# Attention on one core: value products moved to the end of a half step, projections in one piece, and TensorE's program written out

## The chip, the core and the metric

The kernel runs on one core of a Trainium2 chip. The core has five engines that run side by side and meet through semaphores: TensorE (PE; its weight loads are shown apart as PEld), VectorE (DVE), ScalarE (ACT), GpSimd (POOL) and SyncE (SP, which issues the DMAs). The metric is the time of one execution in microseconds, lower is better. A matmul writes its result into one of eight banks of PSUM, and a bank can be used again only when whoever reads it has read it.

## The reference

64 sequences of 128 positions and 256 channels go through two blocks. Each block is a cross attention and a mixture of experts, each with a residual. The change touches only the two attentions. Cut to what matters, one of them is:

```python
q = (layernorm(x) @ Wq + bq).reshape(B, L, H, D)      # H = 16 heads of D = 16
k = (ctx @ Wk + bk).reshape(B, L, H, D)
v = (ctx @ Wv + bv).reshape(B, L, H, D)
scores = einsum('blhd,bshd->bhls', q, k)              # 128 x 128 for each head
scores = where(mask, -inf, scores)
attn = softmax(scores * scale, axis=-1)
out = einsum('bhls,bshd->blhd', attn, v).reshape(B, L, H * D)
x = x + out @ Wo + bo
```

## The kernel before

**Work and its pieces.** The function `attention` is called twice, once for each block. It goes through 32 steps, `p` = 0 to 31. A step holds two sequences, and is done in two halves, `s` = 0 and `s` = 1, one sequence each. The 16 heads of a sequence are four units of four heads, so that a unit's scores (128 queries by 4 x 128 keys) fill one PSUM bank. Several stages overlap: in step `p` the scores of `p` are made, the queries, keys and values of `p+1` and `p+2` are projected, and the output of `p-1` is projected.

**What a half does on TensorE.** `score` writes the mask of all four units (L534 and L538, bf16, on 32 rows of the array) and adds the score products (L548, 32 rows). `turn_n` (L481) turns the normed input of step `p+2` and stands in half 0 only. `turn_p` (L559) turns one unit's probabilities, four 128x128 transposes into the bank that the unit's scores had. `project_q`, `project_k`, `project_v` and `project_o` are groups of fp32 products in three parts each, written by the helper `mm3` (L69, L70 and L71). `times_v` (L572) multiplies the turned probabilities of a unit with the values, on 32 columns of the array. `turn_recip` (L580) turns the reciprocals of the sums. In half `s` the probabilities' units 2 and 3 of the half before ("the late units") are turned first, then units 0 and 1 of the half itself. The value products in a half are those of the half before.

**What the others do.** DVE: `row_max` (L777) takes the extremes of a unit's scores, `keep_p` (L784) copies a unit's turned probabilities to `probsT`, `invert` (L790) the reciprocals, `rest_n` (L760) the low part of the normed input, `keep_o` (L798) copies the raw output, `keep_v` (L769) the values, `residual` (L805) adds to `x`, `stats` (L812) and, in steps 0 to 6 of the first attention, `measure` (L2582) take statistics of `x`. ACT: `exps` (L693) makes a unit's probabilities and their sums, `round_n` (L671) and `round_c` (L676) the high parts of the inputs, `keep_q`, `keep_k`, `norm` the rest. POOL: `normalize`, `spread`, `rest_c`, `add_bo` and `split_q`, which makes the queries' halves that the scores need.

**What sets the order.** Each engine runs its own list in the order in which it is written; there is no scheduler. An instruction whose semaphore has not come stops all that stand behind it on its engine. ACT's list in a step is `keep_k(p+1)`, `round_n(p+2)`, `round_c(p+2)`, four `exps`, `keep_q(p+1)`, `norm(p+3)`, four `exps`. So the first `exps` of half 0 stand behind `round_n`, which waits for TensorE's `turn_n`. And `turn_n` waits for the `residual` of two steps back, because both use bank 7:

```python
wait(pe, x_done, p - 3)                               # in turn_n
wait(pe, exp_done, UP * p + UNITS * s + (u + 1 if u < 2 else UNITS))   # in turn_p
if u == UNITS - 1:
    wait(pe, pT_ready, UP * p + k)                    # the bank of unit 2, read by keep_p
```

TensorE's list is a loop over steps 10 to 27 in the first attention and 2 to 27 in the second (`pairs`, two steps a turn); the other steps, and all steps of DVE, ACT and POOL, are written out.

Of the kernel before, what the change touches and what calls it, by code (L numbers as in the profile page):

```python
# [26 lines left out]
P = 128  # L27
# [34 lines left out]
def is_(index, value):  # L62

    return isinstance(index, int) and index == value
# [301 lines left out]
def attention(nc, S, L, ctx_dram, W, bias, counted, load_next, signals, first, next_norms, next_table, x_dram=None, R=None, X=None):  # L366
# [7 lines left out]
    with ExitStack() as mem:  # L374
        def sb(name, shape, dt=F32):
            return mem.enter_context(nc.sbuf_tensor(f"{L}_{name}", shape, dt))
# [8 lines left out]
        kT = sb("kT", [P, 2, KT, 2 * P])  # L385
        v_pad = sb("v_pad", [P, 2, 2, H * 2 * D + 2 * D])
        probs = sb("probs", [P, UNITS, UH, P])
        probsT = sb("probsT", [P, UNITS, UH, P])
        neg_max = sb("neg_max", [P, 2, UNITS, UH])
        sums, recip = sb("sums", [P, 2, KT, UH, 2]), sb("recip", [P, 2, KT, UH * 2])  # L390
        recip_wide = sb("recip_wide", [P, 2, KT, UH * 2 * D])
# [45 lines left out]
        with nc.Block() as block:  # L437
# [34 lines left out]
            def _(pe):  # L472
# [51 lines left out]
                def score(p, b, s):  # L524
# [11 lines left out]
                    for u in range(UNITS):  # L536
# [1 line left out]
                        pe.matmul(score_bank[s][u][:, :, LATE:], S.late_q16[at, :],  # L538
                                  S.late_k16[at, LATE:].unsqueeze(1).broadcast_to([32, UH, P - LATE]),
                                  start=False, stop=True, skip_group_check=True)  # L540
                    if s == 0:
                        pe.wait_ge(halves_ready, p + 1)
                        pe.wait_ge(kT_ready, p + 1)
                    for i in range(UH):
                        m, e = divmod(i, 2)
                        for u in range(UNITS):
# [15 lines left out]
                def times_v(p, b, k):  # L562

                    s, u = divmod(k, UNITS)
                    m, e = divmod(u, 2)
                    wait(pe, pT_ready, UP * p + k + 1)
                    if u == 0:
                        wait(pe, o_kept, 2 * p + s)
                    if k == 0:
                        pe.wait_ge(v_ready, p + 1)  # L570
                    for i in range(UH):
                        last = pe.matmul(o_ps[32 * i:32 * (i + 1), 0, m, :], v_pad[:, b, s, 32 * (2 * UH * e + UH * m + i):32 * (2 * UH * e + UH * m + i + 1)],  # L572
                                         probsT[:, u, i, :], start=u == 0, stop=True, skip_group_check=True)
                    last.then_inc(pv_done, 1)

                def turn_recip(p, s):
# [6 lines left out]
                def step(p, b):  # L583
                    for s in range(2):
                        before = (p, b, UNITS) if s else (p - 1, 1 - b, UP)
                        exists = s == 1 or not is_(p, 0)
                        score(p, b, s)
                        if s == 0 and more(p, 2):
                            turn_n(p + 2)
                        if exists:  # L590
                            turn_p(before[0], before[2] - 2)
                        if s == 0 and more(p, 1):
                            project_v(p + 1, 1 - b)
                        if s == 1 and more(p, 2):
                            project_k(p + 2, b)
                        if exists:
                            turn_p(before[0], before[2] - 1)
                        for half in range(2):
                            if half:
                                turn_p(p, UNITS * s)  # L600
                                if exists:
                                    for u in range(UNITS, 0, -1):
                                        times_v(before[0], before[1], before[2] - u)
                                turn_p(p, UNITS * s + 1)
                                if exists:
                                    turn_recip(before[0], before[2] // UNITS - 1)
                            if s == 0 and more(p, 1):
                                project_q(p + 1, 1 - b, half)
                            if s == 1 and not is_(p, 0):
                                project_o(p - 1, half)  # L610

                busy(pe, S, 0, 8)
                turn_n(0)
# [7 lines left out]
                turn_n(1)  # L621
                project_k(1, 1)
                pe.wait_ge(wlo_ready, 4)
                pairs(pe, step)
                turn_p(NP - 1, UP - 2)
                turn_p(NP - 1, UP - 1)
                if not first:
# [129 lines left out]
            def _(dve):  # L757
# [21 lines left out]
                def keep_p(p, k):  # L779

                    dve.wait_ge(pT_made, UP * p + k + 1)
                    wait(dve, pv_done, UP * p + k - UNITS + 1)
                    s, u = divmod(k, UNITS)
                    dve.tensor_copy(probsT[:, u], pT_ps[s][u]).then_inc(pT_ready, 1)  # L784

                def invert(p, s):

# [27 lines left out]
                def step(p, b):  # L815
                    for s in range(2):
# [3 lines left out]
                        if s == 0 and not (is_(p, 0) or is_(p, 1)):  # L820
                            residual(p - 2)
                        row_max(p, UNITS * s)
                        if exists:
                            invert(*before)
                            keep_p(before[0], UNITS * before[1] + 2)
                        if s == 0 and more(p, 2):
                            rest_n(p + 2, b)
                        row_max(p, UNITS * s + 1)
                        if exists:
                            keep_p(before[0], UNITS * before[1] + 3)  # L830
                        row_max(p, UNITS * s + 2)
                        if s == 1 and not (is_(p, 0) or is_(p, 1)):
                            stats(p - 2)
                        keep_p(p, UNITS * s)
                        row_max(p, UNITS * s + 3)
                        keep_p(p, UNITS * s + 1)
                        if exists:
                            keep_o(*before)
# [1970 lines left out]
```

## Time and profile before

| what | value |
|---|---|
| time, median of three runs | 2945.97 us (2945.2 to 2952.49) |
| the profiled execution, its own time | 2940.16 us |
| its span | 2938.3 us |
| PE busy over the span | 2775.9 us (94%) |
| DVE busy | 2248.8 us (77%) |
| ACT busy | 1862.7 us (63%) |
| POOL busy | 1566.7 us (53%) |
| TensorE's granted clock, mean | 0.981 |
| first attention, first to last mask | 28.42 to 535.72 us |
| second attention, first to last mask | 2167.65 to 2659.40 us |

The two attentions take about a third of the span. The rows of a timeline give the start from the beginning of the span, the length, the engine, the line, what is written and read, and how many instructions are merged. A matmul's end lies about 0.27 us behind its start and is modelled; the next one starts long before that, so the distance from one row's start to the next is what a group costs, not its length. In brackets stands the idle time of the engine before the row and who ended it.

### The profile page before, as it was taken

The numbers are of one execution on the slowest core, as the hardware profiler recorded it, in microseconds if no ns is written. First come the engines' busy times: TensorE is split into PE (matmuls) and PEld (weight loads), VectorE is DVE, ScalarE is ACT, GpSimd is POOL, SyncE is SP. The second block draws the span as 40 slices with busy tenths as digits, with TensorE's granted clock in tenths as the row PEclk, the third lists the DMA queues.
The fourth block names the chain that finished last, engine by engine and source line by source line (L and its number), as shares of the span: only waits on it lengthen the run. The fifth ranks groups of instructions, "written<-read, shape, count | busy, mean of one in ns | idle before, by whom it ended". The sixth has DMA issues, their size and how long they took to land. (4 is left out here: it accounts for less than half of the span.)

```text
span 2938.3 us, 78905 instructions
## 1 busy us (share of the span) xinstructions
PE 2775.9 (94%) x26882; PEld 2563.4 (87%) x26882; DVE 2248.8 (77%) x6107; ACT 1862.7 (63%) x6875; POOL 1566.7 (53%) x1809
## 2 busy tenths in 40 slices
PE   7999999799999999997999999999989999998686
PEld 6889999689999999996999999999989999995375
DVE  7988888777777777777777777777778888886454
ACT  6889999655555555555444444444479999996233
POOL 4566666567777777775222222222236666665535
PEclk9999999899999999999999999999999999999798
DMA  6000000010000000000000000000010000001243
GB/s 233 17 17 19 18 15 12 8 61 11 11 11 11 11 11 11 11 11 24 30 11 11 11 11 11 11 11 11 1 52 19 19 15 18 19 9 61 93 125 115
DMA packets 56110, 87.23 MB, mean 30 GB/s; under 512 B 6846, under 2 KB 42688, under 8 KB 55104
## 3 DMA queue, kind: packets, MB, share of 16 engines
q1 hardware_dynamic: 49008, 68.01, 7.3%
q0 software_dynamic: 6144, 15.86, 1.5%
q8 instruction: 74, 1.21, 0.2%
q14 instruction: 164, 1.34, 0.2%
q10 hardware_dynamic: 720, 0.79, 0.1%
HBM read 57.75 MB, written 27.94 MB: 29 GB/s over the span
## 5 line engine op out<-in xcount | busy, mean ns | idle before, releaser
L693 ACT ACTIVATE L_probs<-bank,L_neg_max 128x128 f32<-128x128 f32 x2048 | 721.8, 388 | 34.4 <-DVE L_neg_max L777 33.4
L693 ACT ACTIVATION_READ_ACCUMULATOR L_probs<-bank,L_neg_max 128x1 f32 x2048 | 464.3, 227 | 0.0
L784 DVE COPY L_probsT<-bank 128x512 f32<-128x512 f32 x512 | 347.5, 679 | 66.4 <-PE bank L559 44.5
L1927 ACT ACTIVATE M_inter<-bank 128x512 f32<-128x512 f32 x256 | 153.4, 599 | 386.3 <-PE bank L71 386.3
L777 DVE TENSOR_REDUCE L_neg_max<-bank 128x4 f32<-128x512 f32 x512 | 349.4, 683 | 45.5 <-PE bank L548 45.4
L69 PE MATMUL bank<-W_hi,M_nT_hi 128*128 128x384 f32 (+1 forms) x1024 | 363.7, 355 | 9.1 <-DVE M_qkv L1511 4.6
L70 PE MATMUL bank<-W_hi,M_nT_lo 128*128 128x384 f32 (+1 forms) x1024 | 346.4, 338 | 0.0
L71 PE MATMUL bank<-W_lo,M_nT_hi 128*128 128x384 f32 (+1 forms) x1024 | 345.9, 338 | 0.0
L559 PE MATMUL bank<-constants,L_probs 128*128 128x128 f32 x2048 | 319.3, 278 | 16.6 <-DVE L_probsT L784 11.5
L1994 DVE TENSOR_TENSOR M_inter_lo<-M_inter,M_inter_hi 128x512 fp32r<-128x512 f32 x256 | 184.0, 719 | 178.0 <-ACT M_inter_hi L1928 172.8
L69 PE MATMUL bank<-W_hi,M_inter_hi 128*128 128x256 f32 x1024 | 290.6, 284 | 5.3 <-DVE M_inter_lo L1994 4.1
L69 PE MATMUL bank<-M_nT_hi,W_hi 128*128 128x256 f32 x1024 | 293.9, 287 | 0.0
L71 PE MATMUL bank<-M_nT_lo,W_hi 128*128 128x256 f32 x1024 | 290.1, 283 | 0.0
L70 PE MATMUL bank<-M_nT_hi,W_lo 128*128 128x256 f32 x1024 | 289.5, 283 | 0.0
L70 PE MATMUL bank<-W_hi,M_inter_lo 128*128 128x256 f32 x1024 | 287.2, 280 | 0.0
L71 PE MATMUL bank<-W_lo,M_inter_hi 128*128 128x256 f32 x1024 | 286.8, 280 | 0.0
L559 PEld LDWEIGHTS bank<-constants,L_probs 128*128 128x128 f32 x2048 | 228.1, 140 | 54.5 <-issue 38.0
L976 POOL TENSOR_TENSOR L_o<-L_o_raw 128x256 f32<-128x256 f32 x128 | 93.5, 730 | 341.4 <-DVE L_o_raw L798 341.4
L69 PEld LDWEIGHTS bank<-W_hi,M_nT_hi 128*128 128x128 f32 x1024 | 193.6, 189 | 26.1 <-issue 6.3
L2086 POOL TENSOR_TENSOR M_gate_rnorm<-M_gate_squared,constants 128x2 f32<-128x2 f32 x32 | 25.9, 810 | 347.0 <-DVE M_gate_squared L1981 347.0
L1377 ACT ACTIVATE M_qkv_part<-bank,M_rw 128x384 f32<-128x384 f32 x192 | 111.7, 582 | 148.6 <-PE bank L71 148.6
L70 PEld LDWEIGHTS bank<-W_hi,M_nT_lo 128*128 128x128 f32 x1024 | 194.0, 189 | 10.7
(349 smaller groups left out, 9068.2 us busy)
## 6 DMA issues: line engine op xcount, KB each, us to landing
L_ctx_in<-in_ctx SPq DMA_DIRECT2D x64, 256.0 KB, 2.6
M_tile<-M_sorted SPq DMA_DIRECT2D x68, 130.0 KB
raw_weights<-in_weights SPq DMA_DIRECT2D x2, 4096.0 KB, 15.3
hs<-M_hs SPq DMA_DIRECT2D x64, 128.0 KB, 1.7
M_hs<-hs SPq DMA_DIRECT2D x31, 256.0 KB
x_all<-in_x SPq DMA_DIRECT2D x7, 1024.0 KB, 11.0
raw_weights<-in_weights SPq DMA_DIRECT2D x2, 1024.0 KB, 6.7
raw_weights<-in_weights SPq DMA_DIRECT2D x1, 2048.0 KB, 8.7
```

Of the source, the lines that this page charges most:

```text
L69: pe.matmul(out, left[0], right[0], start=first, stop=False)
L70: pe.matmul(out, left[1], right[0], start=False, stop=False)
L71: return pe.matmul(out, left[0], right[1], start=False, stop=last)
L559: last = pe.transpose(pT_ps[s][u][:, i, :], probs[:, k % UNITS, i, :], S.ident[:])
L693: last = act.activation(probs[:, k % UNITS, i, :], score_bank[s][u][:, i, :], ACT.Exp, bias=neg_max[:, s, u, i:i + 1], scale=-1.0, accum_o ...
L777: dve.tensor_reduce(neg_max[:, s, u, :], score_bank[s][u], AX.X, ALU.min).then_inc(max_ready, 1)
L784: dve.tensor_copy(probsT[:, u], pT_ps[s][u]).then_inc(pT_ready, 1)
L976: pool.tensor_tensor(o_sb[:], o_raw[:, s, 0, :], o_raw[:, s, 1, :], ALU.mult)
L1377: act.activation(qkv_part[:, e // 2 - 1, :], q_bank[1], ACT.Copy, scale=rw[:, s % 3, 0, e:e + 1]).then_inc(M.odd_read, 1)
L1927: act.activation(inter[:, e % 2], up_bank[e % 2], ACT.Gelu).then_inc(M.inter_ready, 1)
L1994: dve.tensor_tensor(iT[1][:, e % 2].rearrange("p k t -> p (k t)"), inter[:, e % 2], iT[0][:, e % 2].rearrange("p k t -> p (k t)").bitcast( ...
L2086: pool.tensor_tensor(T.rnorm[:], T.squared[:], S.minus_half[:, 0:T.n], ALU.pow).then_inc(M.rooted, 1)
```

## The change

In `step` on TensorE, each half turned the late units around the first projection, and had half of the query or output projection, then unit 0's turn, the value products, unit 1's turn, the reciprocals and the other half of the projection. Now unit 0's turn stands directly behind the second late unit's, the query or output projection is in one piece, unit 1's turn and the reciprocals follow, and the value products stand last, directly ahead of the next mask. The waits of half 0's scores for the queries' halves and the keys stand ahead of the value products of the half before (for `p` = 0 where they stood).

`probsT` of units 0 and 1 has two buffers, one for even and one for odd halves; the second lies in `sb` in the first attention and in the space of the raw weights in the second. `keep_p` of these units waits for the value products of two halves back. On DVE, `row_max` of unit 1 stands ahead of `keep_p` of the first late unit, `invert` stands behind that `keep_p`, the other extremes move up by one place each, and both `keep_p` of the half's own units stand together. TensorE's steps are all written out. The lists of ACT, POOL and SP are the same as before.

```diff
-        probsT = sb("probsT", [P, UNITS, UH, P])
+        even = sb("probsT", [P, UNITS, UH, P])
+        odd = sb("probsT_odd", [P, 2, UH, P])[:] if first else S.raw[:, E * KT * C:E * KT * C + 2 * UH * P].rearrange(
+            "p (u h q) -> p u h q", u=2, h=UH)
+        probsT = [[even[:, u] for u in range(UNITS)], [odd[:, u] for u in range(2)] + [even[:, u] for u in range(2, UNITS)]]
...
-                    if s == 0:
-                        pe.wait_ge(halves_ready, p + 1)
-                        pe.wait_ge(kT_ready, p + 1)
+                    if s == 0 and is_(p, 0):
+                        pe.wait_ge(halves_ready, 1)
+                        pe.wait_ge(kT_ready, 1)
...
                         if exists:
                             turn_p(before[0], before[2] - 1)
+                        turn_p(p, UNITS * s)
                         for half in range(2):
-                            if half:
-                                turn_p(p, UNITS * s)
-                                if exists:
-                                    for u in range(UNITS, 0, -1):
-                                        times_v(before[0], before[1], before[2] - u)
-                                turn_p(p, UNITS * s + 1)
-                                if exists:
-                                    turn_recip(before[0], before[2] // UNITS - 1)
                             if s == 0 and more(p, 1):
                                 project_q(p + 1, 1 - b, half)
                             if s == 1 and not is_(p, 0):
                                 project_o(p - 1, half)
+                        turn_p(p, UNITS * s + 1)
+                        if exists:
+                            turn_recip(before[0], before[2] // UNITS - 1)
+                        if s == 1 and more(p, 1):
+                            pe.wait_ge(halves_ready, p + 2)
+                            pe.wait_ge(kT_ready, p + 2)
+                        if exists:
+                            for u in range(UNITS, 0, -1):
+                                times_v(before[0], before[1], before[2] - u)
...
-                pairs(pe, step)
+                pairs(pe, step, True)
...
-                    wait(dve, pv_done, UP * p + k - UNITS + 1)
                     s, u = divmod(k, UNITS)
-                    dve.tensor_copy(probsT[:, u], pT_ps[s][u]).then_inc(pT_ready, 1)
+                    wait(dve, pv_done, UP * p + k + 1 - (2 * UNITS if u < 2 else UNITS))
+                    dve.tensor_copy(probsT[s][u], pT_ps[s][u]).then_inc(pT_ready, 1)
...
                         row_max(p, UNITS * s)
+                        row_max(p, UNITS * s + 1)
                         if exists:
+                            keep_p(before[0], UNITS * before[1] + 2)
                             invert(*before)
-                            keep_p(before[0], UNITS * before[1] + 2)
```

TensorE's list before, first attention, half 0, from the second late unit's turn on (bank4). The turn of unit 0 writes bank0, that of unit 1 bank1; L572 are the value products, L580 the reciprocals, and the groups of L69 to L71 into bank7 the two halves of the query projection:

```order
L559 MATMUL bank4<-constants,L0_probs 128x128 x4
L69 MATMUL bank7<-L0_nT_hi,W0_hi 128x256
L70 MATMUL bank7<-L0_nT_hi,W0_lo 128x256
L71 MATMUL bank7<-L0_nT_lo,W0_hi 128x256
L69 MATMUL bank7<-L0_nT_hi,W0_hi 128x256
L70 MATMUL bank7<-L0_nT_hi,W0_lo 128x256
L71 MATMUL bank7<-L0_nT_lo,W0_hi 128x256
L559 MATMUL bank0<-constants,L0_probs 128x128 x4
L572 MATMUL bank5<-L0_probsT,L0_v_pad 32x128 x16
L559 MATMUL bank1<-constants,L0_probs 128x128 x4
L580 MATMUL bank5<-constants,L0_recip_wide 128x128 x2
L69 MATMUL bank7<-L0_nT_hi,W0_hi 128x256
```

The same place now, where the turns have become L562:

```order
L71 MATMUL bank6<-W0_lo,L0_cT_hi 128x256
L562 MATMUL bank4<-constants,L0_probs 128x128 x4
L562 MATMUL bank0<-constants,L0_probs 128x128 x4
L69 MATMUL bank7<-L0_nT_hi,W0_hi 128x256
L70 MATMUL bank7<-L0_nT_hi,W0_lo 128x256
L71 MATMUL bank7<-L0_nT_lo,W0_hi 128x256
```

and, behind the twelve products of the query projection, the end of the half now (L575 are the value products, L537 the next half's mask):

```order
L71 MATMUL bank7<-L0_nT_lo,W0_hi 128x256
L562 MATMUL bank1<-constants,L0_probs 128x128 x4
L583 MATMUL bank5<-constants,L0_recip_wide 128x128 x2
L575 MATMUL bank5<-L0_probsT_odd,L0_v_pad 32x128 x8
L575 MATMUL bank5<-L0_probsT,L0_v_pad 32x128 x8
L537 MATMUL bank0<-constants 128x512
L537 MATMUL bank1<-constants 128x512
```

Unit 0's turn has moved ahead of six more products, and the value products from the middle to the end. VectorE's list before, from `keep_o` of half 0's end (L798) through half 1, where L777 are the extremes, L784 the copies of turned probabilities and L790 `invert`:

```order
L798 COPY L0_o_raw<-bank5 128x512
L769 TENSOR_TENSOR L0_v_pad<-bank6,rows 128x2x8x16 x2
L777 TENSOR_REDUCE L0_neg_max<-bank0 128x4
L790 RECIPROCAL L0_recip<-L0_sums 128x16
L784 COPY L0_probsT<-bank3 128x512
L777 TENSOR_REDUCE L0_neg_max<-bank1 128x4
L784 COPY L0_probsT<-bank3 128x512
L777 TENSOR_REDUCE L0_neg_max<-bank2 128x4
L812 BN_STATS stats<-x_all 128x6 x2
L784 COPY L0_probsT<-bank0 128x512
L777 TENSOR_REDUCE L0_neg_max<-bank4 128x4
L784 COPY L0_probsT<-bank1 128x512
```

and the same stretch now (L803 `keep_o`, L782 extremes, L789 copies, L795 `invert`):

```order
L803 COPY L0_o_raw<-bank5 128x512
L774 TENSOR_TENSOR L0_v_pad<-bank6,rows 128x2x8x16 x2
L782 TENSOR_REDUCE L0_neg_max<-bank0 128x4
L782 TENSOR_REDUCE L0_neg_max<-bank1 128x4
L789 COPY L0_probsT<-bank3 128x512
L795 RECIPROCAL L0_recip<-L0_sums 128x16
L782 TENSOR_REDUCE L0_neg_max<-bank2 128x4
L789 COPY L0_probsT<-bank3 128x512
L817 BN_STATS stats<-x_all 128x6 x2
L782 TENSOR_REDUCE L0_neg_max<-bank4 128x4
L789 COPY L0_probsT_odd<-bank0 128x512
L789 COPY L0_probsT_odd<-bank1 128x512
```

The first copy out of bank3, that of the first late unit, now has two extremes ahead of it instead of one.

## Rows read from the trace of the kernel before

**Rows 1.** Busy times of the engines in the middle of the second attention:

```profile
core 0: us, PE busy (x) PEld busy (x) DVE busy (x) ACT busy (x) POOL busy (x), PEclk, DMA share, GB/s
2200.00:2600.00 400.00, 400.00 (x5896) 362.69 (x5898) 358.43 (x662) 378.88 (x1833) 256.43 (x332) 1.00 0.06 18
```

**Rows 2.** Timeline of PE, step 23 of the first attention, in the loop:

```profile
404.67 0.69 PE L534 MATMUL bank<-constants 32*128 32x512 bf16 x4
...
406.29 0.66 PE L481 MATMUL bank<-constants,L_normed 128*128 128x128 f32 x4
406.79 0.60 PE L559 MATMUL bank<-constants,L_probs 128*128 128x128 f32 x4
...
408.65 0.60 PE L559 MATMUL bank<-constants,L_probs 128*128 128x128 f32 x4
...
409.80 0.60 PE L559 MATMUL bank<-constants,L_probs 128*128 128x128 f32 x4
410.33 1.08 PE L572 MATMUL bank<-L_probsT,L_v_pad 128*32 128x128 f32 x32
411.34 0.66 PE L559 MATMUL bank<-constants,L_probs 128*128 128x128 f32 x4
...
412.86 0.45 PE L534 MATMUL bank<-constants 32*128 32x512 bf16 x4
...
420.38 0.69 PE L534 MATMUL bank<-constants 32*128 32x512 bf16 x4
```

**Rows 3.** Timeline of ACT, same step: first and last instruction of half 0's unit 0:

```profile
408.00 0.36 ACT L693 ACTIVATE L_probs<-bank,L_neg_max 128x128 f32<-128x128 f32 x1
...
409.28 0.22 ACT L693 ACTIVATION_READ_ACCUMULATOR L_probs<-bank,L_neg_max 128x1 f32 x1
```

**Rows 4.** Timeline of DVE, same step:

```profile
404.74 0.68 DVE L798 COPY L_o_raw<-bank 128x512 f32<-128x512 f32 x1
405.34 0.68 DVE L805 TENSOR_TENSOR x_all<-bank,x_all 128x512 f32<-128x512 f32 x1
...
414.36 0.69 DVE L777 TENSOR_REDUCE L_neg_max<-bank 128x4 f32<-128x512 f32 x1 [0.32 <-PE bank L548]
```

**Rows 5.** Timeline of POOL, step 23, `split_q`:

```profile
416.23 2.04 POOL L949 TENSOR_TENSOR L_q_half<-L_q,constants 128x512 f32<-128x512 f32 x2
```

**Rows 6.** Timeline of PE, step 29 of the first attention, written out:

```profile
498.83 0.61 PE L534 MATMUL bank<-constants 32*128 32x512 bf16 x4
...
500.37 0.66 PE L481 MATMUL bank<-constants,L_normed 128*128 128x128 f32 x4
...
506.95 0.39 PE L534 MATMUL bank<-constants 32*128 32x512 bf16 x4
...
508.28 0.66 PE L559 MATMUL bank<-constants,L_probs 128*128 128x128 f32 x4
...
514.42 0.61 PE L534 MATMUL bank<-constants 32*128 32x512 bf16 x4
```

**Rows 7.** Timeline of DVE, then PE: a turn that waits for a copy:

```profile
2648.02 0.63 DVE L784 COPY L_probsT<-bank 128x512 f32<-128x512 f32 x1
...
2648.80 0.63 PE L559 MATMUL bank<-constants,L_probs 128*128 128x128 f32 x4 [1.03 <-DVE L_probsT L784]
```

**Rows 8.** Timeline of ACT, then PE: a turn that waits for probabilities:

```profile
2171.97 0.22 ACT L693 ACTIVATION_READ_ACCUMULATOR L_probs<-bank,L_neg_max 128x1 f32 x1
...
2172.24 0.66 PE L559 MATMUL bank<-constants,L_probs 128*128 128x128 f32 x4 [0.22 <-ACT L_probs L693]
```

**Rows 9.** Timeline of PE, step 4 of the first attention, with statistics on DVE:

```profile
95.68 0.60 PE L534 MATMUL bank<-constants 32*128 32x512 bf16 x4
...
98.47 0.63 PE L481 MATMUL bank<-constants,L_normed 128*128 128x128 f32 x4 [1.20 <-DVE x_all L805]
...
105.03 0.39 PE L534 MATMUL bank<-constants 32*128 32x512 bf16 x4
...
112.55 0.60 PE L534 MATMUL bank<-constants 32*128 32x512 bf16 x4
```

**Rows 10.** Timeline of DVE, same step, `residual`:

```profile
97.66 0.67 DVE L805 TENSOR_TENSOR x_all<-bank,x_all 128x512 f32<-128x512 f32 x1
```

More of the change, by code:

```diff
@@ L572, in times_v @@
                         last = pe.matmul(o_ps[32 * i:32 * (i + 1), 0, m, :], v_pad[:, b, s, 32 * (2 * UH * e + UH * m + i):32 * (2 * UH * e + UH * m + i + 1)],
-                                         probsT[:, u, i, :], start=u == 0, stop=True, skip_group_check=True)
+                                         probsT[s][u][:, i, :], start=u == 0, stop=True, skip_group_check=True)
                     last.then_inc(pv_done, 1)
@@ L822, in step @@
                         row_max(p, UNITS * s)
+                        row_max(p, UNITS * s + 1)
                         if exists:
+                            keep_p(before[0], UNITS * before[1] + 2)
                             invert(*before)
-                            keep_p(before[0], UNITS * before[1] + 2)
                         if s == 0 and more(p, 2):
                             rest_n(p + 2, b)
-                        row_max(p, UNITS * s + 1)
+                        row_max(p, UNITS * s + 2)
                         if exists:
                             keep_p(before[0], UNITS * before[1] + 3)
-                        row_max(p, UNITS * s + 2)
                         if s == 1 and not (is_(p, 0) or is_(p, 1)):
                             stats(p - 2)
+                        row_max(p, UNITS * s + 3)
                         keep_p(p, UNITS * s)
-                        row_max(p, UNITS * s + 3)
                         keep_p(p, UNITS * s + 1)
```

## The prediction, made before the changed kernel ran

> **What bounds the kernel now.** I read first the busy times by stretch, then TensorE's timeline of a step, then the other engines' timelines of the same step, looking for what each waits on. In the middle of the second attention PE is busy for all of 400 us, ACT for 378.88, DVE for 358.43 [rows 1]. So TensorE sets the pace there, with ACT close behind. The looped step takes 15.71 us from mask to mask: half 0 8.19 (404.67 to 412.86), half 1 7.52 (to 420.38) [rows 2]. TensorE stands nowhere in it except where the array changes between its whole, its rows and its columns. Four turns lie 0.11 apart, (0.60 - 0.27) / 3, so the last starts 0.33 after the first, but the value products come 0.53 after it (409.80 to 410.33): a change costs 0.20 instead of 0.11. The last value product starts 0.81 after the first, the turn behind it 1.01 after: 0.20 again, and the second turn comes 0.05 late (its group takes 0.66 against 0.60) [rows 2].
>
> TensorE is the bound because nothing it needs comes late. The question is how much air there is. Unit 0's probabilities in half 0 are made from 408.00 to 409.50 (409.28 + 0.22) [rows 3], and TensorE turns them at 409.80 [rows 2]: 0.3 us of air.
>
> **What goes.** (a) The loop. A written-out step takes 15.59 (498.83 to 514.42) [rows 6] against 15.71: 0.12 a step. (b) In a written-out half 0 the time from the mask to `turn_n` is 1.54, in half 1 that to the first turn is 1.33 [rows 6]; the same mask and scores. The 0.21 are the wait for the copy of unit 1's turned probabilities, which VectorE delivers late. That copy now has the reciprocals and all value products as cover, so the wait goes: 0.21. (c) Array changes. Each half had four (products to mask, scores to turns, turns to value products, back to turns) and has three. Two go, at 0.09 (0.20 less 0.11) and 0.09 + 0.05; one comes, from columns to rows. No row shows that one. Its bounds: 0 (as if it were none), and 0.14 (as the costliest one seen); I take 0.09, the nearest rows' 0.20 less 0.11. So 0.14 a half, 0.28 a step, between 0.18 and 0.46. Without new waits a step would take 15.71 - 0.12 - 0.21 - 0.28 = 15.10.
>
> The Trainium skill (TensorEngine Tiling (Array Packing), Key Properties) says "Changing tiling mode (not just tile) drains the TensorE". By it the change from columns to rows is no cheaper than the others, and the step without new waits would be 15.10; if it did not hold there it would be 14.92. No row of this profile has that change.
>
> **What comes, half 0.** I carry the rows forward from the mask, at 0.
> - The last value product now starts 0.20 before the mask and ends 0.07 after it. `keep_o` waits for it: 0.11, with the 0.04 that a DVE instruction starts behind a matmul in these timelines. In the loop it started at 0.07 [rows 2, 4], but there only VectorE's own work was ahead of it.
> - The next DVE instruction starts 0.60 later [rows 4]: `residual` at 0.71, ended at 1.39. `turn_n` follows 0.14 behind it (98.47 against 97.66 + 0.67) [rows 9, 10]: 1.53. TensorE is free at 1.33, so it stands 0.20.
> - From `turn_n` to the first exponential is 1.71 (406.29 to 408.00), since ACT has the two roundings ahead of it, and a unit takes 1.50 [rows 2, 3]; the turn follows 0.05 behind (2172.24 against 2172.19) [rows 8]. Unit 0 can be turned at 1.53 + 1.71 + 1.50 + 0.05 = 4.79.
> - TensorE is there at 1.53 + 0.50 (`turn_n`) + 1.86 (late unit and value projection, 406.79 to 408.65) [rows 2] + 0.44 (second late unit) = 4.33. It stands 0.46, and a turn after a stand costs 0.05 more. Before, six more products stood ahead, and used the same time.
> - Then turn and whole query projection 1.91, unit 1's turn 0.44, reciprocals to value products 0.11 + 0.20 = 0.31, value products to mask 1.01: 4.79 + 3.67 = 8.46. Half 0 takes 8.46 instead of 8.19.
>
> **What comes, half 1.**
> - The extremes of unit 0 started 1.50 after the mask (414.36 to 412.86) [rows 2, 4], in written-out code 0.06 sooner: 1.44. `keep_o` at 0.11 and `keep_v` (0.66) are done by 1.37, just hidden; if they were not, the chain would move by the lack.
> - Unit 1's extremes now stand ahead of the late unit's copy: it starts at 1.44 + 0.60 + 0.60 = 2.64 and takes 0.69. The second late unit's turn uses the same bank and follows 0.15 behind a copy (2648.80 against 2648.65) [rows 7]: 3.48.
> - TensorE is there at 1.33 + 0.49 + 1.42 = 3.24, where 1.42 are twelve products (1.86 - 0.44). It stands 0.24 and the turn costs 0.05 more: 3.97 at its end. Unit 0's probabilities are ready at 1.44 + 0.68 + 0.03 + 1.50 + 0.05 = 3.70, so this turn doesn't wait.
> - 3.97 + 1.86 (unit 0 and the output projection) + 0.44 + 0.31 + 1.01 = 7.59, instead of 7.52.
>
> Queued behind TensorE's new waits is all of its list; for ACT the roundings, for DVE the last copies. The queries' halves are waited for ahead of the value products, at 6.4 in half 1. They landed at 5.41 (416.23 + 2.04 - 412.86) [rows 2, 5]; `invert` goes one copy and one extreme back, which delays them by at most 1.2 and, as POOL is still at the normalizing then, by about 0.8. I cost it at nothing; if that cover is gone, 0.2 a step. The second buffer for units 0 and 1 is needed for the new order and takes away no wait of its own.
>
> **The sum.** A step takes 8.46 + 7.59 = 16.05: the same from the other side: the 15.10 and three waits, 0.20, 0.46 + 0.05 and 0.24 + 0.05, are 16.10, within rounding. Against the loop that is +0.34, 18 + 26 = 44 times: 15.0. Against the written-out full steps, two in each attention, +0.46 four times: 1.8. In steps 1 to 6 of the first attention four statistics stand ahead of `residual`: it starts 1.98 after the mask instead of 0.67 [rows 2, 4, 9, 10], so each takes 0.33. There half 0 becomes 8.46 + 1.31 = 9.77 against 9.35, and in half 1 two statistics push the extremes from 1.44 to 2.03: 8.18 against 7.52 [rows 9]. That is +1.08, six times: 6.5. The other ten steps, first and last, I give a mean of +0.35: 3.5. Together 27 us. On the profiled execution's 2940.2 that is 2967; the median of the runs lies 5.8 above it, so 2973, and I put 2972.
>
> Bounds: the change of array matters only in half 1, half 0 being a chain that starts at the value products' end; 64 halves by -0.07 (where `keep_v` takes over) or +0.05 are -4 or +3 us. Without the 0.20 at `turn_n`, -13. If the queries' halves are late, +12.
>
> **Rivals.**
> - *TensorE stays the bound.* The new waits don't come about, or nearly: the step takes 15.10, which is 0.61 less, 44 times, 0.49 less four times, and some 0.4 less in the ten first and last steps: 2946 - 27 - 2 - 4 = 2913. For it: TensorE is 100% busy [rows 1], and everything that the change takes away is on it. Against it: 0.3 us of air where 0.8 are used. It decides at 0.61: if the waits of a step are together under that, the kernel is faster. I have 0.95 to 1.0, so a third of them would have to be missing, as if a unit of exponentials came 0.35 sooner.
> - *Half of the waits.* Only the one for unit 0's probabilities holds, since `residual` is in time and the late unit's copy too: 15.10 + 0.51 = 15.61, 0.10 less, and the steps with statistics a little slower: 2941 to 2948, no change.
> - *The written-out list is slow to fetch*, and the gain of 0.12 turns into a loss. Against it: steps of 15.59 are written out already [rows 6]. It would add 0.12 to 0.3 a step, 2978 to 2986.
>
> **Chances.** The forecast, slower by 14 to 36 us, 0.75. TensorE stays the bound, in whole or in good part, 0.14. Half of the waits 0.08. Slow fetch on top 0.03. About 0.3% (9 us) is what a measurement can tell from no change. Slower by more 0.78, within 0.08, faster 0.14. The range leaves out the first rival and a little above: 2950 to 2984.
>
> **What would show it.** In the profile after: half 0 at 8.4 to 8.5 and half 1 at 7.5 to 7.6 in steps 10 to 29; TensorE idle before the turn of unit 0 in half 0 for 0.4 to 0.5 beyond the change of array, ended by ACT's L_probs; before `turn_n` 0.2, ended by DVE's x_all; before the second late unit's turn in half 1 0.2 to 0.3, ended by DVE's L_probsT; none before the mask; TensorE's busy share in the attention under 97%. Wrong would be: a step under 15.7, ACT's exponentials starting sooner than 1.7 after `turn_n`, or `keep_o` not waiting for the value products.

## The result, and the profile after

| | before | changed |
|---|---|---|
| median (four runs each) | 2946.93 us | 2975.65 us |
| lowest to highest | 2945.2 to 2952.49 | 2971.65 to 2981.09 |
| ratio to before, with 95% interval | | 1.0105 [1.0092, 1.0117] |
| span of the profiled execution | 2938.3 us | 2975.5 us |
| PE, DVE, ACT busy | 2775.9, 2248.8, 1862.7 us | 2767.5, 2246.6, 1855.2 us |

The changed kernel is 1% slower, as forecast (2972, range 2950 to 2984), with the same work: the busy times of the three engines in the table are even a little lower. In the changed kernel, lines up to 10 below those of before are the same code: L537 is the mask (before L534), L484 the normed input's turn, L562 the probabilities' turns, L575 the value products, L782 the extremes, L789 the copies.

Busy times of the changed kernel in the middle of the second attention, columns as in [rows 1]:

```profile
core 0: us, PE busy (x) PEld busy (x) DVE busy (x) ACT busy (x) POOL busy (x), PEclk, DMA share, GB/s
2220.00:2600.00 380.00, 366.81 (x5470) 327.79 (x5469) 331.14 (x615) 350.91 (x1710) 240.57 (x309) 1.00 0.07 19
```

TensorE was busy for all of such a stretch before; now it is for 96.5%. The timeline of PE in step 22 of the first attention, to be read beside [rows 2]:

```profile
405.47 0.39 PE L537 MATMUL bank<-constants 32*128 32x512 bf16 x4
...
407.04 0.63 PE L484 MATMUL bank<-constants,L_normed 128*128 128x128 f32 x4 [0.17 <-DVE x_all L810]
...
409.38 0.60 PE L562 MATMUL bank<-constants,L_probs 128*128 128x128 f32 x4
...
410.27 0.66 PE L562 MATMUL bank<-constants,L_probs 128*128 128x128 f32 x4 [0.29 <-ACT L_probs L698]
...
413.40 0.62 PE L575 MATMUL bank<-L_probsT,L_v_pad 128*32 128x128 f32 x16
...
413.95 0.40 PE L537 MATMUL bank<-constants 32*128 32x512 bf16 x4
...
415.28 0.66 PE L562 MATMUL bank<-constants,L_probs 128*128 128x128 f32 x4
...
417.46 1.06 PE L562 MATMUL bank<-constants,L_probs 128*128 128x128 f32 x8
...
421.55 0.40 PE L537 MATMUL bank<-constants 32*128 32x512 bf16 x4
```

A place given as 4.80 or the like is the time in us from the mask of its half. Half 0 takes 8.48 (405.47 to 413.95), half 1 7.60: 16.08 a step, and so in nearly every step that is not first, last or with statistics. Unit 0's turn comes at 4.80, 0.89 after the late unit's, where 0.44 would do: TensorE stands 0.45. The idle time in brackets, 0.29, is smaller than that: a matmul's modelled end lies 0.27 behind its start, and the next would have started 0.11 behind. The group's length of 0.66 instead of 0.60 is the mark of a turn that did not come in a row. The eight turns at 417.46 (second late unit and unit 0) come 2.18 after the first late unit's; 0.49 and 1.42 would be 1.91.

VectorE and ScalarE in the same half 0, to be read beside [rows 3, 4]:

```profile
405.60 0.69 DVE L803 COPY L_o_raw<-bank 128x512 f32<-128x512 f32 x1 [0.43 <-PE bank L575]
406.21 0.68 DVE L810 TENSOR_TENSOR x_all<-bank,x_all 128x512 f32<-128x512 f32 x1
406.94 1.29 DVE L782 TENSOR_REDUCE L_neg_max<-bank 128x4 f32<-128x512 f32 x2
```

```profile
407.70 0.60 ACT L676 ACTIVATE L_nT_hi<-bank 128x512 fp32r<-128x512 f32 x1 [1.21 <-PE bank L484]
...
408.72 0.36 ACT L698 ACTIVATE L_probs<-bank,L_neg_max 128x128 f32<-128x128 f32 x1
...
410.00 0.21 ACT L698 ACTIVATION_READ_ACCUMULATOR L_probs<-bank,L_neg_max 128x1 f32 x1
```

The raw output's copy now waits for the value products and starts 0.13 after the mask; `residual` ends at 406.89, the turn follows at 407.04, the probabilities of unit 0 end at 410.21, their turn follows at 410.27. This is a chain that goes back and forth between three engines: value products (TensorE), copy and `residual` (VectorE), `turn_n` (TensorE), roundings and probabilities (ScalarE), unit 0's turn (TensorE). ScalarE stands 1.21 in it, waiting for `turn_n`; it stood 0.48 at the same place before.

With statistics ahead of `residual` (step 4 of the first attention, beside [rows 9]):

```profile
101.70 0.39 PE L537 MATMUL bank<-constants 32*128 32x512 bf16 x4
...
104.57 0.63 PE L484 MATMUL bank<-constants,L_normed 128*128 128x128 f32 x4 [1.48 <-DVE x_all L810]
...
111.48 0.40 PE L537 MATMUL bank<-constants 32*128 32x512 bf16 x4
...
119.66 0.39 PE L537 MATMUL bank<-constants 32*128 32x512 bf16 x4
```

Half 0 takes 9.78 and half 1 8.18. From the first to the last mask, the first attention takes 527.1 us instead of 507.3 and the second 503.6 instead of 491.8: 31.7 us more together, against 28.7 between the medians. The two profiled executions differ by 37.2: 31.7 in the attentions, 7.7 behind the second one, in code that is the same, and 0.7 ahead of the first mask, while the stretch between the attentions is 3.0 shorter. On the chips of the experiments the stretch behind the second attention takes 216 to 219 us in every run, with TensorE's order of before (e1, e6) as with the others, so nothing there points at the change.

### The profile page after: what moved, and what is told of

It is laid out like the page before. It is cut to its first block and busy times, and to the rows that moved or that the text cites. A ratio compares the mean times of both kernels' runs of the same rounds, so it can differ in the third digit from the quotient of the medians.

```text
span 2975.5 us, 78150 instructions
## 1 busy us (share of the span) xinstructions
PE 2767.5 (93%) x26881; PEld 2546.9 (86%) x26882; DVE 2246.6 (76%) x6107; ACT 1855.2 (62%) x6875; POOL 1569.9 (53%) x1809
## 5 line engine op out<-in xcount | busy, mean ns | idle before, releaser
L698 ACT ACTIVATION_READ_ACCUMULATOR L_probs<-bank,L_neg_max 128x1 f32 x2048 | 501.2, 245 | 0.0
L69 PE MATMUL bank<-W_hi,M_nT_hi 128*128 128x384 f32 (+1 forms) x1024 | 364.3, 356 | 8.7 <-DVE M_qkv L1516 4.8
L562 PE MATMUL bank<-constants,L_probs 128*128 128x128 f32 x2048 | 306.9, 278 | 47.6 <-ACT L_probs L698 21.3
L71 PE MATMUL bank<-W_lo,M_nT_hi 128*128 128x384 f32 (+1 forms) x1024 | 346.2, 338 | 0.0
L782 DVE TENSOR_REDUCE L_neg_max<-bank 128x4 f32<-128x512 f32 x512 | 334.4, 674 | 10.5 <-PE bank L551 7.6
L789 DVE COPY L_probsT<-bank 128x512 f32<-128x512 f32 x384 | 262.5, 684 | 67.1 <-PE bank L562 59.5
L562 PEld LDWEIGHTS bank<-constants,L_probs 128*128 128x128 f32 x2048 | 227.6, 141 | 84.1 <-issue 38.8
L69 PE MATMUL bank<-W_hi,M_inter_hi 128*128 128x256 f32 x1024 | 290.8, 284 | 5.7 <-DVE M_inter_lo L1999 3.2
L69 PE MATMUL bank<-M_nT_hi,W_hi 128*128 128x256 f32 x1024 | 293.6, 287 | 0.0
L71 PE MATMUL bank<-M_nT_lo,W_hi 128*128 128x256 f32 x1024 | 290.0, 283 | 0.0
L71 PE MATMUL bank<-W_lo,M_inter_hi 128*128 128x256 f32 x1024 | 286.9, 280 | 0.0
L69 PEld LDWEIGHTS bank<-W_hi,M_nT_hi 128*128 128x128 f32 x1024 | 193.7, 189 | 25.1 <-issue 5.9
```

The costliest lines, as they stand in the source:

```text
L69: pe.matmul(out, left[0], right[0], start=first, stop=False)
L71: return pe.matmul(out, left[0], right[1], start=False, stop=last)
L562: last = pe.transpose(pT_ps[s][u][:, i, :], probs[:, k % UNITS, i, :], S.ident[:])
L698: last = act.activation(probs[:, k % UNITS, i, :], score_bank[s][u][:, i, :], ACT.Exp, bias=neg_max[:, s, u, i:i + 1], scale=-1.0, accum_o ...
L782: dve.tensor_reduce(neg_max[:, s, u, :], score_bank[s][u], AX.X, ALU.min).then_inc(max_ready, 1)
L789: dve.tensor_copy(probsT[s][u], pT_ps[s][u]).then_inc(pT_ready, 1)
```

## The experiments

Theory: the removals are worth what was worked out, and three new waits outweigh them: `turn_n` for `residual` behind the raw output's copy (0.20), unit 0's turn for its probabilities (0.51), and the second late unit's turn for a copy that has one more reduction ahead (0.29). Rivals: the loss is in the long list of TensorE; or one chain carries all of it; or, with the waits gone, ScalarE is the bound and nothing is won.

The experiments ran on two other chips (e5, e6 and e7 on one, the rest on the other), where the kernel before takes 2880 to 2883 us. In the changed kernel, which has a trace on both the first chip and one of these (e9), what follows the second attention is some 70 us shorter there, and the full steps are the same to 0.02 us. The kernel before has a trace on the first chip alone; its halves below are from there. So ratios are compared, and steps. Each ratio is to runs of before on the same chip.

| kernel | half 0 | half 1 | median | ratio to before, 95% interval |
|---|---|---|---|---|
| before | 8.18 | 7.52 | | 1 |
| changed (e9) | 8.48 | 7.60 | 2904.53 | 1.0084 [1.0071, 1.0098] |
| e1, before, written out | 8.13 | 7.46 | 2875.90 | 0.9980 [0.9970, 0.9989] |
| e2, unit 0's turn later | 8.01 | 7.59 | 2880.55 | 0.9996 [0.9986, 1.0006] |
| e3, late unit's copy first | 8.49 | 7.44 | 2899.91 | 1.0060 [1.0043, 1.0077] |
| e4, residual first | 8.27 | 7.60 | 2889.08 | 1.0031 [1.0022, 1.0041] |
| e5, all three | 8.24 | 7.30 | 2871.99 | 0.9970 [0.9959, 0.9980] |
| e6, e5 with products in the middle | 8.39 | 7.47 | 2884.06 | 1.0006 [0.9997, 1.0015] |
| e7, e5 with the first step's wait back | 8.24 | 7.30 | 2872.88 | 0.9968 [0.9958, 0.9979] |
| e8, e5 and the low part sooner | 7.80 | 7.31 | 2847.92 | 0.9883 [0.9868, 0.9898] |

Halves are those of step 20 of the first attention.

### The written-out list alone (e1)

```diff
-                pairs(pe, step)
+                pairs(pe, step, True)
```

> The kernel before with TensorE's steps written out and nothing else changed. Theory: a step of 15.71 us becomes 15.59, 44 times, so 5 us less than before, about 2942; half 0 still 8.12 with the 0.21 wait between the masks. Rival (a long list is slow to fetch): the steps in the former loop are longer than those that were written out already, over 15.7, and the time is above before.

PE of e1, step 20 of the first attention:

```profile
358.66 0.61 PE L534 MATMUL bank<-constants 32*128 32x512 bf16 x4
...
360.20 0.66 PE L481 MATMUL bank<-constants,L_normed 128*128 128x128 f32 x4
...
366.79 0.39 PE L534 MATMUL bank<-constants 32*128 32x512 bf16 x4
...
374.25 0.61 PE L534 MATMUL bank<-constants 32*128 32x512 bf16 x4
```

A step of 15.59, as forecast, and 5 us less in the median. The wait between the masks is still there (1.54 to `turn_n`, not 1.33). The rival of a slow fetch falls.

### Each wait by itself (e2, e3, e4)

e2, on TensorE:

```diff
-                        turn_p(p, UNITS * s)
                         for half in range(2):
+                            if half:
+                                turn_p(p, UNITS * s)
```

> The changed kernel with unit 0's turn put back between the two pieces of the query or output projection; value products still last. Theory (the wait for unit 0's probabilities is the largest cost): half 0 goes from 8.48 to 7.95, since the turn is reached at 5.04 after the mask and the probabilities are ready at 4.8; half 1 stays at 7.60, where the late unit's copy is what is waited for. Step 15.55, some 58 steps with 0.53 less: 2945. Rival (what costs is the chain from the value products over the output's copy and the residual): half 0 stays over 8.3 and the time over 2965.

e3, on VectorE:

```diff
                         row_max(p, UNITS * s)
-                        row_max(p, UNITS * s + 1)
                         if exists:
                             keep_p(before[0], UNITS * before[1] + 2)
+                        row_max(p, UNITS * s + 1)
+                        if exists:
                             invert(*before)
```

> The changed kernel with VectorE's copy of the first late unit put back ahead of unit 1's extremes, in both halves. Theory: half 1 goes from 7.60 to 7.31, the wait before the second late unit's turn is gone; half 0 stays at 8.48; steps with statistics gain 0.2. 16 us less than the changed kernel: 2959. Rival (half 1 is held by the first exponentials instead): half 1 stays at 7.5 or more, 2970 or more.

e4, on VectorE:

```diff
-                        if s == 0 and not (is_(p, 0) or is_(p, 1)):
-                            residual(p - 2)
...
                         keep_p(p, UNITS * s + 1)
+                        if s == 1 and not is_(p, 0) and more(p, 1):
+                            residual(p - 1)
                         if exists:
                             keep_o(*before)
```

> The changed kernel with VectorE's residual moved ahead of the copy of the raw output, into the end of the half before. Theory: the normed input's turn no longer waits, half 0 goes from 8.48 to 8.28, half 1 stays at 7.60; in the six steps with statistics half 0 goes from 9.79 to about 8.3. 58 times 0.2 and 6 times 1.3: 19 us less than the changed kernel, 2956. Rival (the residual is not on the path outside the steps with statistics): 8.48 stays, and only 9 us are gained, 2967.

PE of e2, half 0 of step 20: the turns of the second late unit, unit 0 and unit 1, between masks:

```profile
363.80 0.40 PE L537 MATMUL bank<-constants 32*128 32x512 bf16 x4
...
367.70 0.60 PE L562 MATMUL bank<-constants,L_probs 128*128 128x128 f32 x4
...
368.85 0.60 PE L562 MATMUL bank<-constants,L_probs 128*128 128x128 f32 x4
...
370.00 0.65 PE L562 MATMUL bank<-constants,L_probs 128*128 128x128 f32 x4
...
371.81 0.40 PE L537 MATMUL bank<-constants 32*128 32x512 bf16 x4
```

Unit 0's turn is reached at 5.05 and does not wait (0.60 long); unit 1's, at 6.20, is 0.05 late, by the mark of 0.65, so it is nearly due itself. Half 0 gains 0.47 of the 0.53. The kernel is level with before: taking out this one wait wins back the whole loss, and it is about half of the three.

PE of e3, half 1 of step 20, with the last row of half 0's unit 0 ahead:

```profile
375.45 0.66 PE L562 MATMUL bank<-constants,L_probs 128*128 128x128 f32 x4 [0.29 <-ACT L_probs L698]
...
379.13 0.40 PE L537 MATMUL bank<-constants 32*128 32x512 bf16 x4
380.46 0.66 PE L562 MATMUL bank<-constants,L_probs 128*128 128x128 f32 x4
...
382.38 1.17 PE L562 MATMUL bank<-constants,L_probs 128*128 128x128 f32 x8
...
386.57 0.40 PE L537 MATMUL bank<-constants 32*128 32x512 bf16 x4
```

The second late unit's turn now comes 1.92 behind the first's, without a wait, as the theory has it. But the eight turns take 1.17 where two units in a row took 1.06: unit 0's probabilities of half 1 are not there yet, and 0.13 are lost again. Half 1 gains 0.16, not 0.29, so the rival is half right: behind the copy, the first exponentials are the next to be waited for. Half 0 stays, with its wait of 0.29 in the row.

PE of e4, step 20:

```profile
360.53 0.40 PE L537 MATMUL bank<-constants 32*128 32x512 bf16 x4
361.86 0.66 PE L484 MATMUL bank<-constants,L_normed 128*128 128x128 f32 x4
...
368.80 0.40 PE L537 MATMUL bank<-constants 32*128 32x512 bf16 x4
...
376.40 0.40 PE L537 MATMUL bank<-constants 32*128 32x512 bf16 x4
```

The turn comes at 1.33, unhindered, and half 0 takes 8.27: minus 0.21. With statistics half 0 is 8.27 too (98.87 to 107.14 in step 4), minus 1.5. The chain over the raw output's copy and `residual` is real, though it is worth less than the turn of unit 0.

By the ratios, e2, e3 and e4 take 25, 7 and 15 us off the changed kernel, where 31, 16 and 19 were expected. Each gain is smaller than its expectation, most of all that of e3, whose interval touches that of the changed kernel: there the steps show the gain, and the total time does not by itself.

### All three, and what came next (e5, e8)

> The changed kernel with all three edits: unit 0's turn between the projection's pieces, the first late unit's copy ahead of unit 1's extremes, the residual ahead of the raw output's copy. Theory (the three waits are all that the change added): half 0 7.75 to 7.85, half 1 7.30 to 7.35, step 15.1, which is what was worked out for the change without new waits; TensorE stands only at changes of the array. 0.6 less than before in 48 steps, more in the steps with statistics: 35 us less than before, ratio 0.988. Rival (ScalarE, whose own work in a step is 14.8, or POOL's queries' halves take over): step 15.3 or more, ratio 0.993 or more.

PE of e5, step 20; then DVE's instruction that it waits for:

```profile
356.39 0.40 PE L537 MATMUL bank<-constants 32*128 32x512 bf16 x4
...
360.08 0.60 PE L562 MATMUL bank<-constants,L_probs 128*128 128x128 f32 x4
360.90 0.39 PE L69 MATMUL bank<-L_nT_hi,W_hi 128*128 128x256 f32 x1 [0.21 <-DVE L_nT_lo L766]
...
364.63 0.40 PE L537 MATMUL bank<-constants 32*128 32x512 bf16 x4
...
371.94 0.40 PE L537 MATMUL bank<-constants 32*128 32x512 bf16 x4
```

```profile
360.21 0.63 DVE L766 TENSOR_TENSOR L_nT_lo<-bank,L_nT_hi 128x512 fp32r<-128x512 f32 x1
```

Half 1 is 7.30, free of waits. Half 0 is 8.24 instead of 7.8, and the ratio 0.997 instead of 0.988. That is as bad as the rival had it, but for another cause. The expectation followed the probabilities, the residual and the copies, but not the low part of the normed input, which the query projection needs. With the late unit's copy first in half 0, VectorE waits for that turn, makes the extremes and the reciprocals, and only then, at 3.82, the low part; the projection comes 0.82 behind a turn, not 0.36. The expectation's theory that three waits are all was wrong by a fourth, which e5's own order made. It was neither ScalarE nor POOL. e8 puts the low part ahead of the reciprocals, and in half 0 unit 1's extremes ahead of the late unit's copy again:

```diff
                         row_max(p, UNITS * s)
+                        if s == 0:
+                            row_max(p, UNITS * s + 1)
                         if exists:
                             keep_p(before[0], UNITS * before[1] + 2)
-                        row_max(p, UNITS * s + 1)
-                        if exists:
-                            invert(*before)
+                        if s == 1:
+                            row_max(p, UNITS * s + 1)
                         if s == 0 and more(p, 2):
                             rest_n(p + 2, b)
+                        if exists:
+                            invert(*before)
```

> The kernel of the three edits; in half 0 VectorE makes the low part of the normed input ahead of the reciprocals, and unit 1's extremes stand ahead of the late unit's copy there as in the changed kernel; half 1 as with the three edits. Theory (half 0 stayed at 8.24 with the three edits because the query projection waited 0.49 for that low part): half 0 7.75 to 7.80, half 1 7.30 to 7.33, step 15.05 to 15.13, 0.45 less than with the three edits in 58 steps, 26 us: ratio to before 0.988. Rival (ScalarE takes over as soon as TensorE is freed): half 0 over 8.0, ratio 0.993 or more.

```profile
350.70 0.40 PE L537 MATMUL bank<-constants 32*128 32x512 bf16 x4
...
358.50 0.40 PE L537 MATMUL bank<-constants 32*128 32x512 bf16 x4
...
365.81 0.40 PE L537 MATMUL bank<-constants 32*128 32x512 bf16 x4
```

7.80 and 7.31: a step of 15.11, against 15.10 worked out before the change ran as that of the change without new waits. The ratio, 0.9883, is the expected one. e8 beats both kernels: 32 us under before and 57 under the changed one. In the middle of its second attention ScalarE is busy for 97% (370.07 of 380 us) and TensorE all the time (columns as in [rows 1]):

```profile
2220.00:2600.00 380.00, 380.00 (x5842) 349.08 (x5844) 347.53 (x654) 370.07 (x1816) 256.26 (x328) 1.00 0.07 19
```

### Where the value products stand (e6), and the first step (e7)

e6 is e5 with TensorE's list of before:

```diff
                             if half:
                                 turn_p(p, UNITS * s)
+                                if exists:
+                                    for u in range(UNITS, 0, -1):
+                                        times_v(before[0], before[1], before[2] - u)
+                                turn_p(p, UNITS * s + 1)
+                                if exists:
+                                    turn_recip(before[0], before[2] // UNITS - 1)
...
-                        turn_p(p, UNITS * s + 1)
-                        if exists:
-                            turn_recip(before[0], before[2] // UNITS - 1)
```

(the value products and the waits that stood at the end of the half go too, and each half 0's scores have these waits).

> The kernel of the three edits with TensorE's order of before put back: value products between unit 0's and unit 1's turns, projection in two pieces around them, the waits for the queries' halves in the scores; all of VectorE's new order, the two buffers and the written-out list stay. Theory (a half gains 0.14 by the products' place, as one change of the array fewer): half 0 7.89, half 1 7.45, step 15.34, 0.28 over that of the three edits, ratio to before 0.992. Rival (the place of the products gains nothing, the gain is all VectorE's order): same step as with the three edits. Second rival (the middle needs unit 1's copy in time): half 0 at 8.1, the wait between the masks is back.

```profile
358.86 0.40 PE L537 MATMUL bank<-constants 32*128 32x512 bf16 x4
...
367.25 0.39 PE L537 MATMUL bank<-constants 32*128 32x512 bf16 x4
...
374.72 0.40 PE L537 MATMUL bank<-constants 32*128 32x512 bf16 x4
```

8.39 and 7.47, against e5's 8.24 and 7.30: the middle costs 0.15 in half 0 and 0.17 in half 1, 0.14 forecast. Both have the wait for the low part, so half 0 is not the 7.89 expected. The wait between the masks is not back. The place of the value products gains some 0.3 a step, 12 us by the medians.

> The kernel of the three edits, with the first step's wait for the queries' halves back in the scores of step 1. Theory: only half 1 of step 0 changes, 8.1 becomes 7.0 in the second attention and about 1 less in the first; 2 us less than with the three edits, which a measurement may just not tell.

```diff
-                    if s == 0 and is_(p, 0):
-                        pe.wait_ge(halves_ready, 1)
-                        pe.wait_ge(kT_ready, 1)
+                    if s == 0 and (is_(p, 0) or is_(p, 1)):
+                        pe.wait_ge(halves_ready, p + 1)
+                        pe.wait_ge(kT_ready, p + 1)
...
-                        if s == 1 and more(p, 1):
+                        if s == 1 and more(p, 1) and not is_(p, 0):
```

Half 1 of step 0 in the second attention was 8.51 in e5 and in e7. The wait for the queries' halves is not what makes it longer than the 7.0 of before. The trace of e7 shows what does:

```profile
2176.72 0.39 PE L537 MATMUL bank<-constants 32*128 32x512 bf16 x1
2177.58 0.39 PE L537 MATMUL bank<-constants 32*128 32x512 bf16 x3 [0.47 <-DVE L_probsT L790]
...
2183.41 0.66 PE L562 MATMUL bank<-constants,L_probs 128*128 128x128 f32 x4 [0.74 <-ACT L_probs L699]
...
2184.22 1.08 PE L575 MATMUL bank<-L_probsT,L_v_pad 128*32 128x128 f32 x32
```

In half 0 of step 0 there are no value products yet, so nothing covers the copy of unit 1's turned probabilities, and the mask stands for it: mask to first turn takes 2.20 instead of the 1.50 of before. And step 0 has no output projection in half 1. Before, the value products filled the time until unit 1's probabilities came; here TensorE stands 0.74 and makes the products afterwards. From unit 0's turn to the next mask that is 3.21 instead of 2.40. The two together are the 1.5.

### The changed kernel once more (e9)

> The changed kernel once more, on the chip of the last kernel, so that both stand against the same runs of before. Ratio to before 1.0105 as measured, on a chip whose last stage is shorter; steps 8.48 and 7.60. If the loss were not in the attention but in the last stage, the ratio would be another here.

1.0084 [1.0071, 1.0098] against 1.0105 [1.0092, 1.0117], 25 us against 29. By the expectation's own words a ratio that differs would point at the last stage; this one is a little lower, and the intervals overlap by a little, so it decides nothing. The masks do: the two attentions of the changed kernel take 1030.7 us on the first chip and 1030.8 here, and on the first chip 31.7 of them are new. The few us that are left between the ratios lie in no stage that the record can name, since before has no trace on this chip.

## Why the prediction was right

| step of the prediction | forecast | measured |
|---|---|---|
| written-out list, a step | -0.12 | -0.12 (e1) |
| wait between the masks | -0.21 | gone: 1.33 to the turn in half 0 of e4 |
| array changes, a half | -0.14 | -0.15, -0.17 (e6 against e5) |
| raw output's copy starts, half 0 | 0.11 | 0.13 |
| `turn_n` | 1.53 | 1.57 |
| `turn_n` to the first exponential | 1.71 | 1.68 |
| unit 0's turn, half 0 | 4.79 | 4.80 |
| late unit's turn, half 1 | 3.48 | 3.51 |
| half 0, half 1 | 8.46, 7.59 | 8.48, 7.60 |
| half 0, half 1 with statistics | 9.77, 8.18 | 9.79, 8.17 |
| the step without new waits | 15.10 | 15.11 (e8) |

**What goes.** All three removals were sized right for the full steps; in step 0 the wait between the masks stays, as e7 showed. The change from columns to rows, which no row of before had, costs what the others do: the last value product starts at 413.75 (413.40 + 0.62 - 0.27) and the mask at 413.95 in the changed kernel, 0.20. The rule of the Trainium skill (TensorEngine Tiling (Array Packing), Key Properties), by which every change of mode drains the array, agrees there.

**What comes.** The three waits are where they were put, and e2, e3 and e4 took each away alone. They don't add: alone they give 0.47, 0.15 and 0.21 a step, against 0.53, 0.29 and 0.20 expected, since behind two of them the next one was due at once. One small thing in half 1 was read wrong: the prediction has `keep_v` done by 1.37 and "just hidden" ahead of the extremes at 1.44. In the changed kernel it ends at 1.48 and the extremes follow without a pause, so `keep_v` sets the start of that chain (step 22, half 1, mask at 413.95):

```profile
414.69 0.74 DVE L774 TENSOR_TENSOR L_v_pad<-bank,rows 128x256 f32<-128x256 f32 x2
415.43 1.29 DVE L782 TENSOR_REDUCE L_neg_max<-bank 128x4 f32<-128x512 f32 x2
```

That is the 0.03 between 3.48 and 3.51 for the late unit's turn. The three waits together, with the low part's order mended, give the 0.97 between 16.08 and 15.11.

**The queries' halves** cost nothing, as costed. POOL's instruction in the changed kernel, beside [rows 5]:

```profile
418.12 2.04 POOL L954 TENSOR_TENSOR L_q_half<-L_q,constants 128x512 f32<-128x512 f32 x2
```

They land at 6.21 after half 1's mask, 0.8 later than before, and the value products start at 6.58.

**The sum.** Forecast 27 us for the attention, 31.7 measured between masks. The 44 looped steps gave 0.37 each nearly everywhere and 15.6 us together (15.0 forecast), the four written-out ones 2.0 (1.8), the six with statistics 6.8 (6.5). The term that was too small is that of the ten first and last steps, taken at a mean of 0.35 without rows of their own: they gave 7.3 and not 3.5. Step 7 gave 1.1, 0.45 of it in half 0 as in steps 1 to 6. Step 8 gave 1.15, and that is a wait that no term has: in half 0 TensorE's turn of the reciprocals stands 0.83 for POOL's `spread` (L971). Step 0 gave 1.7 in the first attention, of which the waits may have only a part, since it is 0.9 longer than before in e1 too (on another chip), and 1.1 in the second. The last step gave 0.6 in each: projections are missing there, so less work of TensorE's own stands ahead of the same inputs (1.52 idle before the late units' turn instead of 1.02, and 0.58 before unit 1's). That the median still lies within 4 us of the forecast is in part luck: forecast and measured differ by 4.7 in the attentions, and the shorter stretch between them and the spread of the runs took some of it back.

**The rivals.** TensorE as the only bound gives 2913 in the forecast; e8, in whose full steps the new waits are gone, lies at a ratio of 0.9883, which on 2946 would be 2912. So the rival's price was right and its condition was not met. "Half of the waits" and the slow list fell with the profile and with e1.

## What to carry to other kernels

When an engine shows no idle time, an order that saves work on it is only as good as the air in front of its inputs: write down for each input when it is ready and when it is used now, and move nothing past that. Here 0.3 us of air stood against 0.8 us used, and a saving of 0.6 us a step became a loss of 0.4. Once one wait is mended the next one may be due at once, so check every input of every moved group, those of the neighbours too; and shorten the chains (the residual ahead of the copy that waits) before giving up the saving.

## What the runs showed of the hardware

The change of TensorE's array between columns (128x32) and rows (32x128) costs 0.20 us from the last matmul's start to the next, as those from and to the whole array do; between transposes in a row on the whole array the distance is 0.11. A loop over two steps of some 230 matmuls each cost 0.12 us a step against the same steps written out, and the written-out list of 32 steps twice was fetched without a wait that the profile shows. On another chip the changed kernel's profiled execution was 73 us shorter (2902.7 against 2975.5), 71 of them behind the last mask of the second attention (216 against 287), while the full steps agreed to 0.02 us. In that last stretch TensorE's granted clock was 0.94 against 0.84 and the DMAs moved 134 against 101 GB/s; which of the two makes the difference is not shown. A difference of kernels is better read from steps than from two medians of different chips.
